# GpSimd issues a group's eight scatters beside attention in one stretch, released by the places alone

## What is computed

```python
scores = jnp.einsum('bhqd,bhkd->bhqk', q, k) / HEAD_DIM ** 0.5
attn = jax.nn.softmax(scores.astype(jnp.float32), axis=-1).astype(scores.dtype)
out = jnp.einsum('bhqk,bhkd->bhqd', attn, v)          # then @ out_w + out_b
...
x = _layernorm(x + attention(x))
res = x
n = layer_norm(x, g1, be1)
x = res + n + (n @ mix_w + mix_b)
res = x
n = layer_norm(x, g2, be2)
probs = jax.nn.softmax(flat @ router_w, axis=-1)
topw, topi = jax.lax.top_k(probs, TOP_K)               # 2 of 8 experts
h = jax.nn.silu(jnp.einsum('td,edf->tef', flat, w1) + b1)
y = jnp.einsum('tef,efd->ted', h, w2) + b2
out = jnp.einsum('te,ted->td', combine, y)
x = _layernorm(x + res + out)
```

## Time and profile before

| what | value |
|---|---|
| median of 3 runs | 1629.66 us (1628.4 to 1630.91) |
| the profiled execution's own time | 1629.42 us |
| its span | 1627.7 us |
| TensorE busy | 1563.8 us, 96% of the span |
| ScalarE busy | 1226.1 us, 75% |
| VectorE busy | 595.0 us, 37% |
| GpSimd busy | 462.1 us, 28% |
| mean granted TensorE clock | 0.988 |

### The profile page before, as it was taken

The page is one execution under the profiler, slowest core; times in us unless marked ns, Lnnn a source line. Parts: engine busy times, 40 slices in busy tenths (PEclk is TensorE's granted clock), DMA queues, the critical chain, the costliest instruction groups (busy, mean ns, idle before and its releaser), DMA issues.

```text
span 1627.7 us, 46348 instructions
## 1 busy us (share of the span) xinstructions
PE 1563.8 (96%) x17759; PEld 931.4 (57%) x17763; DVE 595.0 (37%) x1515; ACT 1226.1 (75%) x1818; POOL 462.1 (28%) x431
## 2 busy tenths in 40 slices
PE   7989999999999999999999999999999999999990
PEld 4444534334344444444344444378899999999990
DVE  6641212554544544445445456343530000000004
ACT  4669999999999999999999999954344334333332
POOL 4730010121221221221221221134545444444441
PEclk9999999999999999999999999999999999999995
DMA  6863310221223462321211211869778776667645
GB/s 167 230 146 82 75 41 19 60 57 35 71 57 77 105 116 58 120 56 39 70 54 41 67 55 41 257 163 193 182 171 234 199 205 183 181 187 193 192 106 213
DMA packets 187563, 195.13 MB, mean 120 GB/s; under 512 B 97161, under 2 KB 159433, under 8 KB 187209
## 3 DMA queue, kind: packets, MB, share of 16 engines
q1 hardware_dynamic: 173587, 174.39, 38.5%
q0 software_dynamic: 13296, 17.77, 6.7%
q10 hardware_dynamic: 495, 0.41, 0.1%
HBM read 141.16 MB, written 47.00 MB: 116 GB/s over the span
## 4 chain that ended last, share of the span: by engine, by line
PE 85%; DVE 3%; issue 2%; ACT 2%; DMA 1%; SPq 0%; POOL 0%; DVEq 0%; POOLq 0%; ACTq 0%
PE at_s L1523 26%; PE at_po L1535 26%; PE at_s L1665 15%; PE at_s L1678 14%; PE at_small L1551 4%; ACT place L1431 2%; DVE late L714 1%; DVE cb_ln_stats L688 1%; DMA at_v<-rows_in 0%; DMA rows_out<-place,at_v 0%; DVE at_o L1754 0%; DMA place<-rows_out 0%; DVE at_den L1764 0%; SPq L1142 0%; PE at_po L1649 0%
## 5 line engine op out<-in xcount | busy, mean ns | idle before, releaser
L1431 ACT ACTIVATE place<-at_s 128x1024 f32<-128x1024 f32 x1024 | 949.8, 1127 | 12.6 <-PE at_s L1523 5.3
L1523 PE MATMUL at_s<-place 99*32 99x512 bf16 x8192 | 570.9, 380 | 7.2 <-PEq L600 5.0
L1535 PE MATMUL at_po<-place,at_v 128*32 128x512 f32 x4096 | 535.5, 593 | 4.3 <-DVE at_o L1754 4.3
L1523 PEld LDWEIGHTS at_s<-place 99*32 99x32 bf16 x8192 | 228.8, 96 | 429.2 <-issue 244.6
L1448 ACT ACTIVATE place<-at_s,b_turned 128x128 f32<-128x128 f32 x568 | 161.6, 368 | 145.2 <-PE at_s L1665 138.9
L1665 PEld LDWEIGHTS at_s<-ex_xT,place 128*128 128x128 f32 x2272 | 264.1, 192 | 6.3 <-issue 2.3
L1665 PE MATMUL at_s<-ex_xT,place 128*128 128x128 f32 x2272 | 265.7, 275 | 0.2 <-issue 0.2
L1678 PE MATMUL at_s<-place 128*128 x1136 | 257.3, 380 | 1.6 <-issue 0.9
L1678 PEld LDWEIGHTS at_s<-place 128*128 128x128 f32 x1136 | 210.4, 190 | 28.3 <-issue 2.6
L1535 PEld LDWEIGHTS at_po<-place,at_v 128*32 128x32 f32 x4096 | 134.8, 110 | 99.3 <-POOL at_v L1269 7.5
L1464 ACT ACTIVATE place<-at_s,at_v 128x256 f32<-128x256 f32 x71 | 33.6, 474 | 161.3 <-PE at_s L1678 151.3
(11 more groups left out here) (219 smaller groups left out, 952.1 us busy)
## 6 DMA issues: line engine op xcount, KB each, us to landing
place<-in_w SPq DMA_DIRECT2D x61, 1024.0 KB, 11.5
place<-in_w SPq DMA_DIRECT2D x72, 256.0 KB
place<-k_parts SPq DMA_DIRECT2D x48, 256.0 KB, 4.4
place<-q_parts SPq DMA_DIRECT2D x186, 64.0 KB
at_v<-rows_in SPq DMA_DIRECT2D x212, 32.0 KB
late<-kept SPq DMA_DIRECT2D x52, 128.0 KB, 2.6
place<-in_x SPq DMA_DIRECT2D x32, 128.0 KB, 3.2
at_heads_T<-at_o SPq DMA_DIRECT2D x128, 32.0 KB
```

The source lines that it names most:

```text
L1431: nc.scalar.activation(probs[:, slot(i, n), :], scores(i, n)[:, :], ACT.Exp).then_inc(exp_done, 1)
L1523: last = nc.tensor.matmul(scores(i, n)[j:j + 32, s * 512:(s + 1) * 512], k_rows[0:ROWS_M, quad(q).start + h, kt * P + j:kt * P + j + 32], ...
L1535: last = nc.tensor.matmul(p_o[32 * h:32 * h + 32, :], v_one[q % 2][:, h, kt, :], probs[:, slot(i, q * NG + g), s * 512:(s + 1) * 512], sta ...
```

## The change

The eight waits for weighing rounds are taken out, and all eight sends stand behind `copy_v` of unit 2. The first still waits for `placed`. `end_sending` stays behind `add_norm`. The sends of groups 6 and 7, among the expert tiles, are as they were.

```diff
-        FIRST_SENDS, LAST_SENDS = (25, 27, 29, 31), (34, 36, 42, 44)
...
-                def send_beside(i, k):
-
-                    pool.wait_ge(weighed, (i + 2) * NR + (FIRST_SENDS + LAST_SENDS)[k] + LEAD)
-                    send(i, k)
-
...
                     copy_v(i * UNITS + 2, (i // QC, 2))
                     if i >= 2:
-                        for k in range(GT):
-                            send_beside(i - 2, k)
+                        for k in range(2 * GT):
+                            send(i - 2, k)
                     copy_v(i * UNITS + 3, (i // QC, 3))
-                    if i >= 2:
-                        for k in range(GT, GT + 2):
-                            send_beside(i - 2, k)
                     add_norm(i - 1)
                     if i >= 2:
-                        for k in range(GT + 2, 2 * GT):
-                            send_beside(i - 2, k)
                         end_sending(i - 2)
```

## The result

The changed kernel takes 1666.86 us (median of 4 runs, 1665.86 to 1667.91) where the kernel before took 1629.03 us beside it (4 runs, 1628.13 to 1630.91): a ratio of 1.0230, 95% interval 1.0217 to 1.0242. It is 38 us slower. I had forecast 1629.5 us and no change, with a range up to 1632.0 us.

What follows compares the result with a forecast made beforehand. The prediction took TensorE to bound the kernel (85% of the chain); six groups of 0, 0 and -0.04 to 0 us summed to -0.2 to 0 us against 1629.42 us, forecasting 1629.5 us, range 1627.2 to 1632.0 us.

Steps and rivals of the forecast that it cites:

- as group 1 had said: Group 1 has no sends, yet L714 takes 2.12 us there; so sends add at most 0.04 us a group.
- the rival built on the Trainium skill's page: VectorE and GpSimd exclude each other at a shared port; L714's stall goes, 3.7 us faster, 1625.8 us; chance 0.04.
- All that I put at nothing by way of buffers, queues and `sent`: Copies queued behind the burst and the earlier `sent` in attention: nobody on the path waits for them, 0 us.
- Four sends more make 0.03 us: Group pitch in attention: 120.54 us with four sends, 120.57 with eight, so scatters cost attention nothing.
- So the burst costs the attention nothing: Eight sends before unit 3's `copy_v`: even the upper bound ends 1.2 us before that copy starts, 0 us.
- The control: Group pitch in the trace before, four sends against eight: 120.54 and 120.57 us, taken as no scatter cost.
- the sum: Six groups of 0 for `copy_v`, 0 for `sent`, -0.04 to 0 for the stretch: -0.2 to 0 us.
- The DMA share: A group's eight sends take 3.4 us of all sixteen DMA engines, covered by loads about 30 us ahead; uncovered 20 us.
- The slower rival: Sends on GpSimd queue until each lands, 8.8 us apart, delaying unit 3's `copy_v`: 74 us, 1703 us; chance 0.04.
- its point of decision: At 6.3 us a send, the eight would end later than unit 3's `copy_v` may start, 557.46 us.
- one unlikely 0.8 us: SyncE's gap before group 7's first expert rows: 0.8 us if all a wait for `sent`, taken as 0.

Runs made afterwards that it cites:

- spread_sends: The changed kernel with an addition of 128 x 256 on GpSimd between one send and the next, sends about 1.8 us apart: 1629.29 us (ratio 1.0002).
- the five jobs: The five sets of follow-up runs, each on a different chip, with variants of the kernel before or the changed one; measured from 1628.78 to 1705.37 us.
- four_four: The changed kernel with one wait put back, so each group's sends go as 4 and 4: 1629.16 us, on another chip 1664.06 us.
- third job: Three earlier programs rerun unaltered beside the changed kernel on another chip: x_full8 1662.58, four_four 1664.06, x_tiny8 1663.6, changed kernel 1662.57, kernel before 1629.47 us.
- a_full4: The changed kernel with four extra indirect scatters of zeros back to back in a later quiet stretch of groups 2 to 6: 1678.34 us.
- x_full8: The kernel before with eight extra back-to-back scatters of zeros behind the next group's first value copy, groups 2 to 6: 1628.95 us, on another chip 1662.58 us.
- late8: The changed kernel with all eight real sends moved, still back to back, behind the copy of the next group's first values: 1670.46 us (ratio 1.0252).
- from25: The changed kernel with the first send's wait for weighing round 25 put back, the other seven directly behind: 1672.89 us (ratio 1.0272).
- spent_waits: The changed kernel with an already fulfilled wait, for weighing round 17, ahead of each send: 1676.34 us (ratio 1.0290).
- aside_early: late8 plus eight extra back-to-back scatters of zeros where the changed kernel sends, in groups 2 to 6: 1705.37 us (ratio 1.0468).
- x_tiny8: x_full8 with rows of 2 elements instead of 256 in the extra scatters: 1628.9 us, on another chip 1663.6 us.

## Why the prediction was wrong

**What was right.** The change does what it says: the first send starts 0.43 us after the cast ends (516.20 to 516.63 us; I took 0.4). The burst is 10.3 us long, as forecast; most sends stand 1.27 us apart, and one that takes 1.35 us brings the mean to my 1.33. `copy_v` of unit 3 is released by TensorE and not by a send, the next copy no longer by a DMA, and L714 takes 2.13 us with no send beside it (the last ended at 526.90 us), so it was not the sends that stretched it, as group 1 had said. That also settles the rival built on the Trainium skill's page "SBUF — State Buffer", section "SBUF: two separate sides": a send beside L714 was not what stretched it, and with the send gone TensorE still waits 0.57 us there. All that I put at nothing by way of buffers, queues and `sent` is nothing: `spread_sends` has the same order and the same releases, and its time is that of before.

**The step that failed** is the one that I wrote as "Four sends more make 0.03 us. Had the scatters a cost for attention in either direction, it would be here", and with it "So the burst costs the attention nothing". The control was sound for what it held: scatters with about 2.5 us of idle time or more between them (2.49 and 2.68 us). The change takes away just that distance. I carried a result from a pitch of 3.5 us to one of 1.27 without a row beside attention at that pitch; the only close ones, the pairs among the expert tiles, served me for the duration and told nothing of the neighbours. The burst, which the sum has at 0, measured 5.9 us a group, and 7.5 in group 2: 37 us in all, not 0.

**Why I did not see it.** I priced what a burst can hold by what the profile names: buffers, GpSimd's queue behind it, transfers. The resource that ran short, the rate at which TensorE gets to start its instructions, has no row in a trace in which it never ran short. The DMA share I had bounded at 3.4 us a group, and I covered it with loads that come 30 us ahead. That cover held, and no load was waited for.

**The slower rival** had the right sign and the wrong mechanism. A send is not slow (0.96 us each) and GpSimd does not queue. I gave it 6.3 us a send as its point of decision and was blind to a cost that another engine pays while GpSimd runs freely. The range, 1627.2 to 1632.0 us, was made of jitter and one unlikely 0.8 us. A situation that no row of before shows, eight scatters back to back beside an engine with no idle time, should have widened it upward.

**What stays open.** Shown: the loss falls on TensorE's issue, inside rounds, without a semaphore; it takes indirect scatters, back to back; it does not depend on place, bytes, contents or waits; it depends on the chip, or on something else that goes with a job, such as where its programs and tensors lie in memory, which the five jobs don't separate.

Not shown is the link. The Trainium skill's page "Runtime: NRT & Kernel Launch", section "Instruction fetch mechanics", says that each engine's instructions come by DMA in blocks of 16 KiB. The trace agrees with the size for one of its two instruction queues: `q8` moves 128 packets of 2.10 MB together, in both kernels. The page also says that the cost of crossing a block is mostly hidden. A slow supply of instructions could look like these rows, but nothing in the trace points to it: from 518.5 to 530.5 us no packet of an instruction queue was under way in the changed kernel. From the packet before that gap to the one behind it (516.76 to 530.61 us) TensorE started 117 matmuls and 112 weight loads, and in the next two such intervals 136 and 132, then 124 and 120, so the next block came no later by count than elsewhere.

How the loss adds up is open too. Four cost 2.0 us and eight 5.9, which would fit two that are free and 1.0 us for each further one. `four_four` in the third job, with two fours 14 us apart, lost 5.8 us a group and not 4.0 (its copies of unit 3 stand 126.3 us apart, against 120.55). Each of its groups has 3.4 us at half clock, as in the last section. If these cost their full 1.7 us, 4.1 us is left, about twice what four cost in `a_full4`; this sum is an estimate.

## What to carry to other kernels

Don't issue a row of indirect scatters back to back beside a TensorE that has no idle time: at a pitch of 1.27 us four cost 2.0 us and eight 5.9 us (two or three were not measured), and at 1.81 us eight cost nothing, so waits that look idle can be what keeps them apart. Read the number of instructions started in a stretch, not the busy share; here 4.09 of 5 us busy was 35 matmuls in place of 78. A control from the trace before covers only the spacing it has, and a null from one job on one chip only that job.

## What the runs showed of the hardware that I had not expected

The same program was free in one job and cost 2% in another, on another chip (`x_full8`: 1628.95 and 1662.58 us), while the kernel before took 1628.9 to 1629.7 us in every job.

Plain DMAs from GpSimd are issued 0.54 us apart (8 in 4.35 us) and leave TensorE alone; indirect ones at half that rate don't, even with rows of 8 bytes.

After a stall of this kind TensorE's granted clock can fall to half, the 1.2 GHz of its two levels. It stands in the last row of `x_full8` in the third job above (0.59). In the changed kernel it happened behind one burst, in group 2:

```profile
402.00:406.00 4.00, 4.00 (x40) 1.32 (x36) 0.00 (x0) 3.21 (x5) 0.00 (x0) 0.60 0.00 0
```

A clock of 0.60 over 4 us is 3.2 us at half clock, worth 3.2 / 2 = 1.6 us, which is what group 2 lost more than the others. In `late8`, `from25`, `spent_waits`, `aside_early` and the second runs of `four_four` and `x_tiny8` such stretches of 3.4 to 6.8 us come back in most groups. Those of them with eight back to back lose 6.8 to 7.8 us a burst on average (41.0 us for six in `late8`, 46.9 us for six in `spent_waits`), against 6.3 in the changed kernel.
